# A state-space, attention and routed feed-forward kernel: the columns of h2 by VectorE block transposition and a DRAM scratch instead of by TensorE

## Time and profile before

| what | value |
|---|---|
| median of 3 runs | 535.89 us |
| the profiled execution's own time | 535.71 us |
| its span, first to last instruction | 533.9 us |
| TensorE matmul (PE) busy | 486.2 us, 91% |
| TensorE weight load (PEld) busy | 407.1 us, 76% |
| VectorE (DVE) busy | 411.5 us, 77% |
| ScalarE (ACT) busy | 255.9 us, 48% |
| GpSimd (POOL) busy | 125.7 us, 24% |
| mean granted TensorE clock | 0.983 |

### The profile page before, as it was taken

The page is one execution under the profiler, slowest core; times in us unless marked ns, Lnnn a source line. Parts: engine busy times, 40 slices in busy tenths (PEclk is TensorE's granted clock), DMA queues, the critical chain, the costliest instruction groups (busy, mean ns, idle before and its releaser), DMA issues.

```text
span 533.9 us, 7434 instructions
## 1 busy us (share of the span) xinstructions
PE 486.2 (91%) x2467; PEld 407.1 (76%) x2467; DVE 411.5 (77%) x866; ACT 255.9 (48%) x469; POOL 125.7 (24%) x110
## 2 busy tenths in 40 slices
PE   3257978889899999999999999999999999999995
PEld 2155757778687888888887888787888888888884
DVE  7989866898787987888787878788988878764241
ACT  3763385947263554646463626263644546323200
POOL 0577952630020303030303020020303030303020
PEclk9996989989999999999999999999999999999999
DMA  8994013021212121221203031212121211212011
GB/s 298 400 294 101 1 46 118 1 83 45 79 47 79 44 79 44 61 62 39 83 19 88 17 88 35 79 44 79 44 79 46 79 41 41 79 35 84 1 39 39
DMA packets 28763, 40.82 MB, mean 76 GB/s; under 512 B 10760, under 2 KB 21192, under 8 KB 28744
## 3 DMA queue, kind: packets, MB, share of 16 engines
q1 hardware_dynamic: 28368, 40.49, 25.1%
q10 hardware_dynamic: 376, 0.10, 0.1%
HBM read 23.80 MB, written 16.78 MB: 76 GB/s over the span
## 4 chain that ended last, share of the span: by engine, by line
PE 36%; DVE 35%; issue 17%; ACT 9%; POOL 1%; DVEq 1%; DMA 0%; ACTq 0%; POOLq 0%
PE acc_b L455 15%; PE acc_a L455 13%; DVE b_sb L1127 4%; PE turnp L448 2%; DVE tmp L1093 2%; DVE tmp L1112 2%; PE turnp L439 2%; DVE x_lo L1174 2%; ACT x_hi L715 2%; ACT x_hi L680 2%; DVE b_sb L1111 2%; PE small L479 1%; DVE st L1135 1%; PE acc_b L420 1%; DVE wa_raw L1015 1%
## 5 line engine op out<-in xcount | busy, mean ns | idle before, releaser
L917 POOL TENSOR_TENSOR h<-h,st 128x1024 f32<-128x1024 f32 x16 | 30.3, 1894 | 337.7 <-PE turnp L448 337.7
L455 PE MATMUL acc_a<-wa_hi,x_hi 128*128 128x512 f32 x256 | 84.1, 405 | 0.5 <-DVE h L1145 0.5
L455 PE MATMUL acc_b<-wb_hi,x_hi 128*128 128x512 f32 x256 | 84.5, 406 | 0.0
L455 PE MATMUL acc_a<-wa_lo,x_hi 128*128 128x512 f32 x256 | 81.6, 395 | 0.0
L455 PE MATMUL acc_b<-wb_lo,x_hi 128*128 128x512 f32 x256 | 81.3, 394 | 0.0
L455 PE MATMUL acc_a<-wa_hi,x_lo 128*128 128x512 f32 x256 | 81.2, 393 | 0.0
L455 PE MATMUL acc_b<-wb_hi,x_lo 128*128 128x512 f32 x256 | 80.9, 392 | 0.0
L455 PEld LDWEIGHTS acc_a<-wa_hi,x_lo 128*128 128x128 f32 x256 | 48.8, 190 | 10.6
L455 PEld LDWEIGHTS acc_b<-wb_hi,x_lo 128*128 128x128 f32 x256 | 48.5, 189 | 10.6
L455 PEld LDWEIGHTS acc_b<-wb_lo,x_hi 128*128 128x128 f32 x256 | 48.5, 189 | 10.5
L455 PEld LDWEIGHTS acc_a<-wa_lo,x_hi 128*128 128x128 f32 x256 | 48.8, 191 | 10.1
(11 more groups left out here) (201 smaller groups left out, 913.9 us busy)
## 6 DMA issues: line engine op xcount, KB each, us to landing
h<-rows_out SPq DMA_DIRECT2D x16, 512.0 KB, 3.2
out<-h SPq DMA_DIRECT2D x15, 512.0 KB
rows_out<-b_sb SPq DMA_DIRECT2D x56, 128.0 KB, 2.3
mask_raw<-in_L_attn_mask SPq DMA_DIRECT2D x8, 512.0 KB, 9.8
wa_raw<-in_L_attn_weight SPq DMA_DIRECT2D x8, 512.0 KB, 10.5
wb_raw<-in_L_ffn_W_base SPq DMA_DIRECT2D x8, 512.0 KB, 14.7
rows_out<-tmp SPq DMA_DIRECT2D x8, 128.0 KB, 2.3
xn<-in_x SPq DMA_DIRECT2D x15, 64.0 KB
```

The lines of the kernel that those rows point to most:

```text
L455: return pe.matmul(cols, a, rows, start=first, stop=last)
L917: pool.tensor_tensor(h2[par][:, :], h2[par][:, :], st2[:, par, 1:2].to_broadcast([P, L]), ALU.subtract)\
```

## The change

The transposes of h2 leave TensorE. `h2_turn` on VectorE transposes the centred h2 in 32 x 32 blocks into tmp, with the eight chunks innermost; four DMAs write tmp to a second DRAM scratch and one reads it back as x2_raw, contraction row on the partition, data row times 8 plus chunk on the free axis. `h2_high` and `h2_low` read it with a step of 8 elements. x2_hi is written in the old layout, x2_lo over x2_raw in place, so that a chunk of x2_lo is read by TensorE with a step of 8 elements (`turned_chunks`). The b tables' second factor moves from tmp to turnp, as does the v tables'. GpSimd's add_bias(t) is moved from step t+1 to step t, after v_factors(t+2). The gated transpose moves from chunk 6 to chunk 5. A reciprocal deviation becomes three VectorE instructions instead of five, and one more on ScalarE. The order of VectorE, ScalarE and SyncE in a step is changed. In the first tiles h2_turn(0) stands after wb_lows(8) and h2_turn(1) after k_turn(2).

```diff
-        x2_hi, x2_lo = sb("x2_hi", [P, KC, P], FR), sb("x2_lo", [P, KC, P], FR)
+        x2_hi = sb("x2_hi", [P, KC, P], FR)
+        x2_raw, x2_lo = sb_twice("x2_raw", [P, L], F, "x2_lo", [P, KC, P])
...
+        def turned_chunks(lo):
+
+            return lo[:, :, :].rearrange("p k n -> p (k n)").rearrange("p (n k) -> p k n", k=KC)
...
+            def h2_columns_write(t):
+
+                sp.wait_ge(h2_turned, t + 1)
+                for g in range(G):
+                    sp.dma_start(h2_cols_out[:, :, g, :].rearrange("q f x -> f q x"),
+                                 tmp[g * 32:(g + 1) * 32, :].rearrange("f (q x) -> f q x", q=Q)).then_inc(turned_out, 16)
+
+            def h2_columns_read(t):
+
+                if later(t, 1) and not at(t, TILES - 1):
+                    sp.wait_ge(ffn_ready, t)
+                sp.dma_start(x2_of(t)[2][:, :], h2_cols_out.rearrange("q f g x -> (q f) (g x)")).then_inc(h2t_in, 16)
...
             def step(t, par):
                 if real(t + 3):
                     load_x(t + 3)
+                h2_columns_write(t)
                 if real(t + 1):
-                    k_rows(t + 1)
+                    k_rows_write(t + 1)
+                    k_rows_read(t + 1, written(t))
+                else:
+                    sp.wait_ge(turned_out, written(t) - OUT)
+                h2_columns_read(t)
                 sp.wait_ge(out_ready, t)
                 store(t - 1, 1 - par)
...
             def step(t, par):
-                pe.wait_ge(kt_turned, t + 1)
-                h2_transposes(t - 1, 1 - par)
                 pe.wait_ge(kt_lo, t + 1)
                 for k in range(KC):
                     attention(t, k)
-                pe.wait_ge(h2t_lo, t)
                 if real(t + 1):
                     k_transposed(t + 1)
+                pe.wait_ge(h2t_lo, t)
                 pe.wait_ge(hwt_lo, t - 1)
                 lora_router(t - 1)
                 pe.wait_ge(out_ready, t - 1)
                 for k in range(KC):
                     if k == 2 and real(t + 2):
                         x_transposes(t + 2)
-                    if k == KC // 2 and at(t, TILES - 1):
-                        h2_transposes(t, par)
-                    if k == KC - 2:
+                    if k == KC - 3:
                         gated_transpose(t - 1)
...
-                act.wait_ge(h2t_ready, t + 1)
-                act.activation(x2_of(t)[0][:, :, :].rearrange("p k n -> p (k n)"), turnp[:, :], ACT.Copy)\
-                    .then_inc(h2t_hi, 1)
+                act.wait_ge(h2t_in, (t + 1) * 16)
+                hi, _, raw = x2_of(t)
+                act.activation(hi[:, :, :], raw[:, :].rearrange("p (n k) -> p k n", k=KC), ACT.Copy).then_inc(h2t_hi, 1)
...
             def step(t, par):
-                act.wait_ge(ffn_ready, t - 1)
-                h2_high(t - 1)
+                if real(t + 2):
+                    x_rows_twice(t + 2)
                 k_sum(t)
                 k_deviation(t)
+                h2_high(t - 1)
                 if real(t + 2):
-                    x_rows_twice(t + 2)
                     exp_and_sin(t + 2)
...
             def add_bias(t, par):
-                pool.wait_ge(h2t_ready, t + 1)
                 pool.wait_ge(h2_dev, t + 1)
+                if real(t + 2):
+                    pool.wait_ge(v_chain, (t + 2) * V_STEPS + 3)
+                else:
+                    pool.wait_ge(h2_turned, t + 1)
...
             def step(t, par):
-                add_bias(t - 1, 1 - par)
+                add_bias(t, par)
...
+                dve.wait_ge(turned_out, written(t - 2))
                 dve.wait_ge(v_ready, t + 1)
                 dve.wait_ge(b_chain, t * 3 + 1)
                 dve.tensor_tensor(whole(b_sb), *b_factors(t, 0), ALU.mult)
-                dve.tensor_tensor(b_terms(tmp), *b_factors(t, 1), ALU.mult).then_inc(b_chain, 2)
+                dve.tensor_tensor(b_terms(turnp), *b_factors(t, 1), ALU.mult).then_inc(b_chain, 2)
...
-                dve.tensor_scalar(s[:, 4:5], s[:, 2:3], 1.0 / L, LN_EPS, ALU.mult, ALU.add)
                 dve.reciprocal(s[:, 5:6], s[:, 3:4]).then_inc(s_chain, 1)
...
+                dve.tensor_scalar(s[:, 6:7], s[:, 4:5], s[:, 5:6], s[:, 3:4], ALU.mult, ALU.add).then_inc(s_chain, 1)
+                dve.wait_ge(s_chain, t * 3 + 2)
+                dve.reciprocal(s[:, 7:8], s[:, 6:7]).then_inc(s_chain, 1)
...
             def h2_low(t):
                 dve.wait_ge(h2t_hi, t + 1)
-                hi, lo = x2_of(t)
-                dve.tensor_tensor(lo[:, :, :].rearrange("p k n -> p (k n)"), turnp[:, :],
-                                  hi[:, :, :].bitcast(F).rearrange("p k n -> p (k n)"), ALU.subtract)\
-                    .then_inc(h2t_lo, 1)
+                hi, lo, raw = x2_of(t)
+                dve.tensor_tensor(turned_chunks(lo), raw[:, :].rearrange("p (n k) -> p k n", k=KC),
+                                  hi[:, :, :].bitcast(F), ALU.subtract).then_inc(h2t_lo, 1)
+
+            def h2_turn(t, par):
+
+                dve.wait_ge(h2_centred, t + 1)
+                dve.wait_ge(turned_out, 2 * OUT if at(t, 0) else written(t - 1))
+                dve.transpose(tmp[:, :].rearrange("p (q r k) -> p q k r", q=Q, k=KC),
+                              h2[par][:, :].rearrange("p (k q f) -> p q k f", k=KC, q=Q)).then_inc(h2_turned, 1)
...
             def step(t, par):
+                if real(t + 1):
+                    table_b(t + 1)
+                if real(t + 2):
+                    phases(t + 2)
+                h1_reciprocal(t)
                 h2_low(t - 1)
+                dve.wait_ge(out_stored[par], t * 8 - 8 * par)
+                attention_residual(t, par)
                 h2_reciprocal(t - 1, 1 - par)
...
+                    k_low(t + 1)
+                h2_turn(t, par)
+                gates(t - 1, 1 - par)
                 if real(t + 1):
-                    k_low(t + 1)
                     k_turn(t + 1)
-                gates(t - 1, 1 - par)
                 if real(t + 2):
                     v_factors(t + 2)
+                gated_low(t - 1)
+                if real(t + 2):
                     table_v(t + 2)
-                gated_low(t - 1)
```

More of the change, by code:

```diff
@@ L176, in build_vit_tower @@
             "attn_ready", "rs1_chain", "h2_ready", "h2_mean", "h2_centred", "h2_square", "h2_dev", "rs2_chain"))
[L177 to L178 removed]
+        h2t_hi, h2t_lo, cat_ready, gate_chain, hw_ready = (sem(n) for n in (
+            "h2t_hi", "h2t_lo", "cat_ready", "gate_chain", "hw_ready"))
         hwt_ready, hwt_hi, hwt_lo, ffn_ready, bias_added, out_ready = (sem(n) for n in (
@@ L295, in x2_of, with written @@
         def x2_of(t):
-            return (x1_hi, x1_lo) if at(t, TILES - 1) else (x2_hi, x2_lo)
+            return (x1_hi, x1_lo, x1_raw) if at(t, TILES - 1) else (x2_hi, x2_lo, x2_raw)
+        def turned_chunks(lo):
+            return lo[:, :, :].rearrange("p k n -> p (k n)").rearrange("p (n k) -> p k n", k=KC)
+        OUT = 16 * Q
+        def written(t):
+            return 3 * OUT + OUT * 2 * t
         def x1_of(t):
@@ L311, in load_x, with k_rows_write, k_rows_read @@
                 sp.dma_start(xn[:, :, :].rearrange("p n r -> p (n r)"), x_v[t]).then_inc(x_in, 16)
-            def k_rows(t):
+            def k_rows_write(t):
+                if at(t, 1):
+                    sp.wait_ge(h1_in, t * 16)
                 sp.wait_ge(kt_turned, t + 1)
+                for q in range(Q):
+                    sp.dma_start(k_rows_out[:, :, q * 256:(q + 1) * 256].rearrange("g r x -> r g x"),
+                                 turned_of(t)[q * 32:(q + 1) * 32, :].rearrange("r (g x) -> r g x", g=G))\
+                        .then_inc(turned_out, 16)
+            def k_rows_read(t, out_count):
                 if at(t, 1):
                     sp.wait_ge(h2_ready, t)
[L318 to L322, removed]
+                sp.wait_ge(turned_out, out_count)
+                sp.dma_start(h1[:, :], k_rows_out.rearrange("g r l -> (g r) l")).then_inc(h1_in, 16)
+            def h2_columns_write(t):
[7 more added lines that the diff above has]
+                sp.dma_start(x2_of(t)[2][:, :], h2_cols_out.rearrange("q f g x -> (q f) (g x)")).then_inc(h2t_in, 16)
             sp.dma_start(ldt[:, :], log_dt).then_inc(ldt_in, 16)
@@ L341, in _ @@
             load_x(3)
-            k_rows(2)
+            k_rows_write(2)
+            h2_columns_write(1)
+            k_rows_read(2, written(1))
+            h2_columns_read(1)
             load_x(4)
@@ L442, in k_transposed @@
                 mm.then_inc(kt_ready, 1)
[L444 to L449, removed]
             def product_part(acc, n, a, w, k, first, last):
@@ L455, in product_part, with x2_chunks @@
                 return pe.matmul(cols, a, rows, start=first, stop=last)
+            def x2_chunks(t, k):
+                x_hi, x_lo, _ = x2_of(t)
+                return x_hi[:, k, :], turned_chunks(x_lo)[:, k, :]
```

(13 more changed lines are left out.)

65 lines of the change are left out of this document (28 added, 37 removed).

## The result

The changed kernel takes 546.38 us (median of 4 runs, 545.17 to 547.22); the kernel before, on the same chip, 536.32 (535.52 to 536.78). The ratio is 1.0188, with a 95% interval of 1.0169 to 1.0207: slower, clear of the noise. The forecast was 526.7, with a range of 518 to 535, so it had the sign wrong.

A forecast was written before the change was run, and what follows sets the result against it. TensorE's issue was taken as the bound, 28.50 us per tile. Transposes -13.1, waits -6.6, router loads +6.5, first pass +3.2 and end +1.0 made -9.0 from 535.71: 526.7 us, range 518 to 535.

The forecast's parts named there:

- The transposes' 0.87 us: TensorE, each loop step: removing the eight h2 transposes saves 0.87 us per tile, -13.1 us over 15 tiles.
- the 0.33 us of the experts' wait: TensorE ahead of the experts: the wait for hw_lo goes altogether, saving 0.33 us per tile.
- The 6.6 us for all such waits: TensorE, whole run: the removed waits for hw_lo ahead of the experts sum to -6.6 us.
- The stepped load: TensorE's x2_lo weight loads: 54 ns more each, 0.43 us per tile in the router (+6.5 us), nothing in base.
- Rival 3: TensorE's base product doesn't hide the stepped load, so 24 loads per tile pay; slower, 541 us; chance 0.08.
- rival 2: TensorE's stepped load doubles, 107 ns more: another +6.5 us, 533.2 us; chance 0.15 together with the surviving wait.
- So I charge no stall: VectorE beside GpSimd's two operations (4.3 us): the new order avoids stalls, so none was charged.
- The first pass, +3.2: TensorE before the first loop pass's router: waits about 3 us for late h2_low; +3.2 us, 0 to 5.
- The end, +1.0 by h2(15)'s round trip: Last tile: nothing covers h2(15)'s trip through DRAM, so TensorE waits 0.6 to 3 us; +1.0 taken.
- VectorE's step, 25.6 us of 27.7: VectorE's work per loop step: 25.6 us, with h2_low at 2.17, fits TensorE's period of 27.7 us.
- Rival 4: VectorE becomes the bound through dearer h2_low or h2_turn, or mis-timed waits; 537 us; chance 0.10.
- ScalarE's h2_high at 1 to 2 us: ScalarE in the loop: the stepped read takes 1 to 2 us, hidden in front of a wait of over 2.

The follow-up runs named there:

- before_gates: The kernel before, with only gated_low put ahead of the v table and the gated transpose one chunk earlier; 532.15 us, ratio 0.9891.
- plain_lo: The changed kernel with x2_lo contiguous again, so TensorE loads it without a step; 530.84 us, ratio 0.988 to the kernel before.
- plain_pool: plain_lo with waits keeping GpSimd out of VectorE's way at four places, and lb_hi made earlier; 522.18 us, ratio 0.9705.
- after_pool: The changed kernel, stepped x2_lo kept, with the GpSimd waits and earlier lb_hi of plain_pool added; 540.65 us, ratio 1.0073.
- plain_order: plain_pool with load_x(4) issued earlier, ScalarE's h2_high before k_sum and VectorE's h2_low before phases; 528.52 us, ratio 0.9833.

## Why the prediction was wrong

By stretches of TensorE, in span: up to attention(2) forecast 0, measured +2.7. From there to router(1) +3.2, measured +4.1. To attention(14) 11.6 passes at -0.77 = -8.9, measured -0.5; in it are 1.96 us of wait that the kernel before had ahead of experts(1), and the 1.85 us that the clock took. From there to the end what is left of -9.0, so -3.3, measured +4.4. Together -9.0 and +10.7.

- **The transposes' 0.87 us and the 0.33 us of the experts' wait: right.** before_gates has the second alone (0.37), plain_lo both: 28.50 - 27.23 = 1.27. The 6.6 us for all such waits were 5.1.
- **The stepped load, taken at +54 ns in the router and at nothing in base: the step that failed.** A load takes 129 ns longer (191 to 320). The router paid 0.93 us per tile instead of 0.43, above the upper bound of 0.86; base 0.32 instead of 0. The 54 ns came from L399, whose plain form takes 141 ns and not 191: another kind of load, shorter to begin with. The bound for base was also thin: 120 + 107 = 227 in a slot of 228 "fits, just". 0.04 us per chunk shows that it didn't quite; the trace doesn't say where in the slot the time goes. In the time, the term of +6.5 us was 15.5 (546.38 to 530.84), about half of the 19.7 us by which the forecast was off. Rival 3 had this mechanism at a chance of 0.08 with 541 us; rival 2 had the router's share. Neither had both.
- **"So I charge no stall": right for the loop, wrong for the ends.** The loop's rows show none. But the forecast followed only step(t) with t+2 real. The trace before already held the case at the start: its wait at the gated transpose of tile 0 is 3.22 us, and its gates end with GpSimd's additions there too (102.65 + 1.89 = 104.54 and 104.62 + 2.42 = 107.04):

```profile
103.28 1.28 DVE L1159 SCALAR_TENSOR_TENSOR gs<-cat,st,bias_r 128x8 f32<-128x8 f32 x1
...
105.00 2.13 DVE L1162 TENSOR_TENSOR gate<-gate,gs 128x64 f32<-128x64 f32 x1
...
108.50 0.33 PE L487 MATMUL small<-kst,hw_sb 128*128 128x128 f32 x1 [3.22 <-DVE hw_sb L1168]
```

In the last two tiles add_bias hangs on h2_turned instead of the v factors and falls onto the gates: 0.79 and 1.31 us of waits. h2_low(0) now reads two SBUF tiles (before, one and PSUM), which put it under GpSimd's table_b(2). The forecast also had nothing for the clock behind a wait; the rows above show 1.85 us for one.
- **The first pass, +3.2: right in place, the size in part luck** (3.91 us waited, +4.1 in all). The stretch began 2.7 us late, which hid some of it: in plain_pool, where attention(2) starts at 112.51, the same stretch takes 18.61 us against 12.69 before the change, so +5.9, above the "5 at most". The queue named was VectorE's, and it was free at 131.54; behind it came 0.95 us more for x2_hi, which ScalarE's wait for load_x(4) had made late. Moving that load gave 1.0 us back.
- **The end, +1.0 by h2(15)'s round trip:** not there in the changed kernel, since the late gates held TensorE longer; it came out once they were gone, as 0.87 us in after_pool and 1.90 in plain_pool, within the forecast's 0.6 to 3.
- **VectorE's step, 25.6 us of 27.7: right.** plain_lo holds 27.23 with h2_low at 2.18, close to the 2.17 of the row taken. Rival 4 didn't happen.
- **ScalarE's h2_high at 1 to 2 us:** 2.17, hidden in the loop. At tile 0 it stands in front of wb_highs(13), and no row shows that it cost time there: VectorE takes the remainder of that chunk up at 90.80, right behind its phases. The wait of 1.87 us ahead of router(0) hangs on h2_low(0), which ends at 94.86, and on the remainder behind it.

## What to carry to other kernels

Before an operand that is loaded as weights gets a new layout, price the load by itself with both layouts at the clock and shape of the product. With 16 bytes or more between elements a load takes some 120 to 135 ns longer here. Of that TensorE pays 0.116 us per load beside the router's short matmuls (0.93 / 8) and 0.02 beside those of 512 columns (0.32 / 16). With 8 bytes it costs nearly nothing. Walk a changed wait condition through the first and the last passes too: an instruction that moved beside harmless work in the loop can lie beside two-operand work there. Remove a wait only after asking which one stands just behind it: plain_order got its router early and paid at the gates. And look at the clock behind a wait of TensorE: the wait can cost more than its own length.

## What the hardware showed that was not expected

- Loads of a 128 x 128 fp32r operand: 188 to 191 ns contiguous, 194 to 199 with a step of 2 elements, 309 with 4, 317 to 323 with 8.
- STREAM_TRANSPOSE of 128 x 1024 from SBUF takes 1.24 us where its output runs are contiguous and 2.18 us with a step of 8.
- ScalarE's copy of 128 x 1024: 1.06 us without a step, 2.17 us with a step of 8 in its source.
- While GpSimd's tensor_tensor on two SBUF tiles runs, small VectorE operations on two SBUF sources wait for its end (0.23 us becomes 1.56, 0.22 becomes 2.16), and of a large pair each waits for the other's (2.14 becomes 3.46, 1.93 becomes 3.67). Transpositions beside it are not held up (2.15 and 2.17 us beside add_bias(0) in plain_pool).
